# Decoder self-attention of a transformer block: another order of VectorE's row maxima and subtractions within a batch

## What is computed

```python
def _L1_attn_ref(x, w_qkv, w_proj, b_proj):      # 16 heads of 8 features
    Q, K, V = split(x @ w_qkv)
    Q, K = apply_rope(Q), apply_rope(K)
    attn = einsum('bqhd,bkhd->bhqk', Q, K) * scale
    attn = where(causal, attn, -1e9)
    attn = softmax(attn, axis=-1)
    return einsum('bhqk,bkhd->bqhd', attn, V) @ w_proj + b_proj
x = _layernorm(x + _L1_attn_ref(...))
```

## Time and profile before

| | us |
|---|---|
| runs (3) | 1361.73, 1365.23, 1362.21 |
| median | 1362.21 |
| span of the profiled execution | 1363.6 |
| PE busy / share of the span | 1199.7 / 88% |
| DVE busy / share | 1041.1 / 76% |
| ACT busy / share | 863.3 / 63% |
| POOL busy / share | 553.3 / 41% |

### The profile page before, as it was taken

How to read it: one execution, slowest core, us unless ns; L and a number is a source line. 1 busy time by engine, 2 the same in 40 slices (tenths; PEclk the granted TensorE clock), 3 DMA queues, 4 the chain that set the end, 5 groups by cost and what they waited for, 6 DMA issues and landing times. The chain is left out here.

```text
span 1363.6 us, 31925 instructions
## 1 busy us (share of the span) xinstructions
PE 1199.7 (88%) x10209; PEld 819.7 (60%) x10209; DVE 1041.1 (76%) x3184; ACT 863.3 (63%) x2474; POOL 553.3 (41%) x831
## 2 busy tenths in 40 slices
PE   3789999999999999988489988999999979999796
PEld 2456666666666666654256655555555556777796
DVE  3477888887888888885678867999999975666365
ACT  2677887878887878864246643666666654543464
POOL 1233334425353434432400017556655311556377
PEclk9999999999999999987589988999999999999899
DMA  6100000000000000000122222013100000000673
GB/s 267 52 17 9 17 15 21 29 17 29 15 31 17 26 19 17 13 15 13 53 67 81 82 71 98 24 39 79 43 24 18 5 1 3 17 17 25 178 209 92
DMA packets 71490, 63.54 MB, mean 47 GB/s; under 512 B 10510, under 2 KB 61586, under 8 KB 70688
## 3 DMA queue, kind: packets, MB, share of 16 engines
q1 hardware_dynamic: 62768, 45.27, 11.5%
q0 software_dynamic: 6400, 12.63, 3.0%
q10 hardware_dynamic: 2160, 3.60, 0.8%
HBM read 43.00 MB, written 18.98 MB: 45 GB/s over the span
## 5 line engine op out<-in xcount | busy, mean ns | idle before, releaser
L777 PE MATMUL e_bank_turned<-c_matrices,e_probs 128*128 128x128 f32 x1024 | 166.0, 286 | 16.2 <-ACT e_probs_t L1009 9.0
L703 POOL TENSOR_TENSOR e_rstd<-e_var_eps,c_minus_half 128x1 f32<-128x1 f32 x128 | 71.0, 570 | 253.6 <-DVE e_var_eps L1050 253.3
L1009 ACT ACTIVATE e_probs_t<-e_bank_turned 128x512 f32<-128x512 f32 x256 | 154.9, 605 | 16.0 <-PE e_bank_turned L777 14.5
L1137 DVE TENSOR_REDUCE e_neg_max<-e_bank_scores 128x4 f32<-128x512 f32 x160 | 109.5, 684 | 50.6 <-PE e_bank_scores L820 50.2
L777 PEld LDWEIGHTS e_bank_turned<-c_matrices,e_probs 128*128 128x128 f32 x1024 | 116.7, 145 | 39.9 <-issue 16.1
L787 PE MATMUL e_bank_mix<-e_probs_t,e_values 128*32 128x128 f32 x2048 | 113.2, 294 | 15.5 <-ACT e_probs_t L1009 15.1
L968 ACT ACTIVATE e_probs<-e_scores,e_neg_max 128x128 f32<-128x128 f32 x384 | 123.2, 410 | 1.1 <-DVE e_neg_max L1173 1.1
L1784 ACT ACTIVATE d_probs_t<-d_bank_turned 128x512 f32<-128x512 f32 x128 | 77.4, 605 | 65.9 <-PE d_bank_turned L1661 65.9
L963 ACT ACTIVATE e_probs<-e_scores 128x512 f32<-128x512 f32 x128 | 82.1, 642 | 42.0 <-DVE e_scores L1170 41.4
L706 POOL TENSOR_TENSOR e_k_by_place<-e_q_k_k,c_matrices 128x512 f32<-128x512 f32 x64 | 66.6, 1040 | 102.6 <-DVE e_q_k_k L1181 102.6
L1766 ACT ACTIVATE d_probs<-d_scores 128x512 f32<-128x512 f32 x128 | 80.8, 631 | 38.9 <-DVE d_scores L1807 38.5
(11 more groups left out here) (328 smaller groups left out, 3267.4 us busy)
## 6 DMA issues: line engine op xcount, KB each, us to landing
streamed<-in_s_up SPq DMA_DIRECT2D x36, 258.0 KB, 3.4
sorted_rows<-scratch_sorted SPq DMA_DIRECT2D x72, 64.0 KB, 1.8
scratch_expert_out<-m_y SPq DMA_DIRECT2D x72, 64.0 KB, 1.5
sorted_rows<-scratch_sorted SPq DMA_DIRECT2D x40, 65.0 KB, 3.0
e_x_in<-in_x SPq DMA_DIRECT2D x32, 64.0 KB, 1.9
e_ctx_in<-in_ctx SPq DMA_DIRECT2D x32, 64.0 KB, 2.1
up<-in_m_wgv SPq DMA_DIRECT2D x1, 2048.0 KB, 7.5
up_b<-in_m_bgv SPq DMA_DIRECT2D x1, 2048.0 KB, 14.1
```

Source lines behind the costliest of these rows:

```text
L777: last = nc.tensor.transpose(turned_bank[:, j * P:(j + 1) * P], pr[k % 3][:, j, :], c["ident"][:])
L1009: nc.scalar.activation(pt[k % 2][:], turned_bank[:], ACT.Copy).then_inc(probs_t_ready, 1)
L1137: nc.vector.tensor_reduce(nmax[k % 4][:], bank, AX.X, ALU.max, negate=True).then_inc(max_ready, 1)
```

## The change

Only DVE's queue in `phase_decode` is written in another order. The instructions are the same, and so are the semaphores that they wait for and signal; the four pairs of a batch are laid out anew over its ticks.

```diff
             for tick in TICKS:
-                if 0 <= tick < UNITS_ALL:
-                    b, g = divmod(tick, G)
-                    dve.wait_ge(scores_done, b + 1)
-                    bank = quad[:, g, :].rearrange("p (j u) -> p j u", j=G)
-                    nc.vector.tensor_reduce(nmax[tick % 4][:], bank, AX.X, ALU.max, negate=True).then_inc(max_ready, 1)
-                    dve.wait_ge(max_ready, tick + 1)
-                    if tick >= 4:
-                        dve.wait_ge(probs_ready, tick - 3)
-                    nc.vector.tensor_tensor(sc[tick % 4][:], bank, bcast(nmax[tick % 4][:], P), ALU.add).then_inc(shifted, 1)
+                inside, g = 0 <= tick < UNITS_ALL, tick % G
+                if inside and g == 0:
+                    largest(tick)
+                    largest(tick + 1)
+                    shift(tick)
+                if inside and g == 1:
+                    shift(tick)
+                    largest(tick + 1)
+                if inside and g == 2:
+                    largest(tick + 1)
+                    shift(tick)
+                if inside and g == 3:
+                    shift(tick)
                 if (b := due(tick, 8)) is not None:
                     dve.wait_ge(mix_back, b + 1)
```

More of the change, by code:

```diff
@@ L1796, in _, with bank_of, largest, shift @@
             chain = Chain(dve, links, 0, 0)
-            for tick in TICKS:
-                if 0 <= tick < UNITS_ALL:
-                    b, g = divmod(tick, G)
-                    dve.wait_ge(scores_done, b + 1)
-                    bank = quad[:, g, :].rearrange("p (j u) -> p j u", j=G)
-                    nc.vector.tensor_reduce(nmax[tick % 4][:], bank, AX.X, ALU.max, negate=True).then_inc(max_ready, 1)
-                    dve.wait_ge(max_ready, tick + 1)
-                    if tick >= 4:
-                        dve.wait_ge(probs_ready, tick - 3)
-                    nc.vector.tensor_tensor(sc[tick % 4][:], bank, bcast(nmax[tick % 4][:], P), ALU.add).then_inc(shifted, 1)
+            def bank_of(u):
+                return quad[:, u % G, :].rearrange("p (j u) -> p j u", j=G)
+            def largest(u):
+                dve.wait_ge(scores_done, u // G + 1)
+                nc.vector.tensor_reduce(nmax[u % 4][:], bank_of(u), AX.X, ALU.max, negate=True).then_inc(max_ready, 1)
+            def shift(u):
+                dve.wait_ge(max_ready, u + 1)
+                if u >= 4:
+                    dve.wait_ge(probs_ready, u - 3)
+                nc.vector.tensor_tensor(sc[u % 4][:], bank_of(u), bcast(nmax[u % 4][:], P), ALU.add).then_inc(shifted, 1)
+            for tick in TICKS:
+                inside, g = 0 <= tick < UNITS_ALL, tick % G
[11 more added lines that the diff above has]
+                    shift(tick)
                 if (b := due(tick, 8)) is not None:
```

## The result

| | kernel before | change |
|---|---|---|
| median of runs, us | 1363.61 (1361.73 to 1365.23, 4 runs) | 1380.07 (1376.17 to 1381.05, 4 runs) |
| ratio, 95% interval | | 1.0099 [1.0071, 1.0127] |
| span of the profiled execution, us | 1363.6 | 1374.3 |
| its mean granted clock | 0.964 | 0.962 |

The change is slower, by more than I forecast: 1380.07 us against 1369.5, and above my range. The other three runs of the change had a mean clock of 0.956 or 0.957. In a later comparison (experiment e5) the same kernel came out at a ratio of 1.0061 [1.0034, 1.0088]; my forecast was 1369.5 / 1362.21 = 1.0054. So the direction and the mechanism stand, and two things are missing from the sum.

The account below looks back on a forecast made before the run. PE's chain with its detour over DVE was taken as the bound. Losses of 5.3 us (batches 5 to 29), 1.0 (batches 2 to 4) and 1.0 (last two) added 7.3 to 1362.2: 1369.5 us, range 1364.0 to 1373.0.

Parts of the forecast that it names:

- What bounds the kernel: Steady batches: PE's chain with its detour over DVE's reciprocal and `d_mix` sets the 8.83 us period; faster DVE buys nothing.
- The stalls between a maximum and its subtraction: DVE's queue: four stalls of 0.11 us removed, 0.43 us of DVE time per batch, priced at nothing.
- The second maximum ahead of the reciprocal: Batches 5 to 29: reciprocal starts at 1.82 instead of 1.61 us, losing 0.21 us per batch, 5.3 us in all.
- Batches 2 to 4: Early batches: reciprocal moves from 1.50 to 1.82 us behind the first maximum, costing 3 × 0.32 = 1.0 us.
- The first subtraction: Subtraction and ACT's first exp 0.49 us later; covered in steady batches, costing 2 × 0.49 = 1.0 us in batches 30 and 31.
- What arrives earlier: Subtractions 1 to 3 and the norms' block come about 0.5 us earlier; nobody waits for them, so nothing gained.
- Rival A: DVE's queue is the bound, so the removed stalls save 12.9 us: 1349.3 us, chance 0.04.
- rival B: PE's chain absorbs the later `d_mix`; only the last batches' 1.0 us remains: 1363.2 us, chance 0.09.
- rival C: ACT's late exp costs 0.49 us in each of 30 batches, 14.7 us: 1376.9 us, chance 0.04.

Follow-up runs that it names:

- e5: The changed kernel itself, with no edit, run again in a second group beside the kernel before: 1373.08 us, ratio 1.0061.
- e9: Kernel before with only DVE reordered: reciprocal still third, rotation behind maximum 2, two of four stalls gone; PE's queue unchanged: 1363.39 us, ratio 0.9998.
- e6: Kernel before with PE's masks of banks 0 and 1 moved ahead of turn 1, bank 2's ahead of L1725: 1358.5 us, ratio 0.9949.
- e1: The change cut to one part: only the second maximum ahead of first subtraction and reciprocal, units 2 and 3 as before: 1371.25 us, ratio 1.0037.
- e7: Changed kernel with PE's masks of banks 0 and 1 moved ahead of turn 1, bank 2's ahead of L1725: 1358.69 us, ratio 0.9948.
- e10: Changed kernel with subtraction 1 moved up too, so two maxima and two subtractions precede the reciprocal: 1386.83 us, ratio 1.0171.
- e2: Changed kernel with one dummy addition on GpSimd ahead of each pair of gathers, to start them later: 1370.53 us, ratio 1.0032.
- e4: Kernel before with one dummy addition on GpSimd ahead of each pair of gathers: 1368.03 us, ratio 1.0020.
- e11: Changed kernel with a dummy GpSimd addition ahead of the gathers and five dummy PE matmuls in each of the last two batches: 1367.76 us, ratio 1.005.
- e3: Changed kernel with five dummy matmuls where PE idles in each of the last two batches: 1371.7 us, ratio 1.0038.
- e12: Kernel before with PE's masks early, DVE reordered with the reciprocal third, and a dummy GpSimd addition ahead of the gathers: 1351.92 us, ratio 0.9926.

## Why the prediction was right and wrong

**What bounds the kernel: right.** PE's chain with its detour over the reciprocal set the period, DVE did not. The Trainium skill ("Perfetto Trace Analysis", "Identifying the Most-Contended Engine") would have named DVE by its occupancy; the runs speak against it: e9 and the change relieve DVE and gain nothing, e6 moves masks on PE and gains 0.31 us per batch.

**"The stalls between a maximum and its subtraction": right**, at nothing (e9). The durations were right too: three instructions ahead put the reciprocal at 1.80, four at 2.40, so 0.60 us each, against 0.73 in a dependent pair. The Trainium skill ("VectorE: DVE Perf Modes", "The DRAIN you can't avoid") found with eight copies in a row that a semaphore after each costs nothing extra; for the pairs here the trace disagrees.

**"The second maximum ahead of the reciprocal": right.** 0.19 us per batch against 0.21 forecast, in the change, in e1 and in e7; a second dose of 0.60 came through in full (e10).

**"Batches 2 to 4": right**, 0.9 against 1.0.

**"The first subtraction": place right, size too large.** At full clock batch 30 grew by 0.29 us (e5, 8.41 against 8.12), not 0.49. The weigh did start 0.46 later, and with it turn 0; 0.2 us of it came back at ACT's copy of turn 0. In the kernel before ACT was still busy there with exp 1 (1100.79 to 1101.42), so that the copy started 0.24 us behind the end of turn 0; in e5 exp 1 was done early and the copy started 0.03 behind it. That is the earlier subtraction 1 at work, which I had priced at nothing in the next paragraph.

**"What arrives earlier" was the step that failed.** I wrote "Nothing". I had looked at who waits for the earlier results and found nobody, which holds for the masks; exp 1 came earlier to some use in batch 30 (above). GpSimd waits for the norms, though, and its gathers moved forward by 0.5 us. The change touches no instruction of GpSimd, but it shifts when they run. The second gather's end then fell 0.07 us ahead of the end of PE's queries and keys, and PE's signal for these was late by 0.45 us, 0.14 us of which reached the period: 21 × 0.14 = 3 us (2.7 against the kernel before, which has three early batches of 8.9 us itself). e2, e4, e10 and e11 show it from four sides.

**A term for the clock was missing.** The sum took the clock to be the same before and after, and by size this is the larger miss. In the profiled execution 1.6 us of batch 30 (9.98 against 8.41) and probably most of the 2.7 us from batch 31 to the end are stretches at half clock (e5 has 18 us of them there instead of 27 and takes 257.5 us instead of 261.0, the kernel before 258.2). The runs of the kernel before in the third group tell what the clock is worth: 1359.12 to 1359.29 us at a mean of 0.970, 1367.38 and 1367.45 at 0.961, some 0.9 us per thousandth. The change's other three runs in the result, at 0.956 and 0.957 against 0.962 in the profiled one, fit this with their 3.4 to 4.9 us more. An estimate from these rows: of the 16.5 us between the medians of the result, 6 are the forecast's terms as measured (25 × 0.19 + 0.9 + 2 × 0.29), 3 the held signal, and 0.0075 less clock (0.9565 against the 0.964 of the profile before) is worth some 7. For e5, whose early period is 9.12, the first two give 8 us, and 7.7 us lie between its medians. Whether the change lowers the clock is **open**. For it: low clock in batch 30 in the change, e2 and e10, which idle there, and not in the fed e3 and e11. Against it: e1 and e5 idle just as much and have none in batch 30 (8.41), e5's seven runs range over 0.958 to 0.970, and the kernel before ranges over 0.959 to 0.971 beside it. The larger ratio of the result may be no more than this spread over four runs.

Rival A fell with e9, rival B with the flat 9.02 of e11, rival C with e1 (late exp in every batch, period no longer than the reciprocal explains).

## What to carry to other kernels

When an edit makes an engine run ahead, list not only who waits for its results but whose *issue times* move, DMA queues on GpSimd included, and what these will then stand beside. Price a reordering by what it puts ahead of the one instruction through which the critical chain passes; here 0.6 us of independent DVE work cost 0.6 us per batch where the chain had no slack, and removing stalls elsewhere on DVE paid nothing. Before calling a loss of less than 1% understood, compare at equal granted clock, and more than once.

## What was unexpected of the hardware

A completion signal of PE that falls due near the end of an indirect DMA instruction on GpSimd can be held until about half a microsecond behind that end. PE itself goes on. In the change the signal of queries and keys was due 0.07 us behind the second gather's end (3.59) and came 0.49 to 0.57 behind it, in all 21 batches; the signal of the values (L1710), due 0.3 behind the end, came with it. In e4 turn 0's was due up to 0.43 us behind the end and came 0.51 to 0.60 behind. A signal that falls due while the gather still runs can be held as well: in e4 weigh 3's was due at 4.05, the gather ended at 4.20 to 4.30 in batches 5 to 14, and the signal came at 4.71 to 4.83. On time were, in all 21 batches, signals due 0.56 us behind the end or later (turn 0 before, 4.63; e10, 0.66 behind).

Nearness to the end is not enough, though. In the kernel before weigh 3's signal was due within 0.04 us of the gather's end, in e9 0.2 behind it, in e12 turn 0's 0.1 behind it, and none of them was held. Batches 3 and 4 of the change had the same gathers as the later ones and an on-time rotation (3.69), but late values (ACT's copy of them at 4.14 and 4.16, against 3.91 in batches 26 to 28). And in e2 weigh 3's signal, due 0.29 behind the end, was held in all 21 early batches (it came 0.51 to 0.63 behind), and the period stayed 9.02, since nobody stood waiting for it. What decides is open; whether the instruction, its descriptors or the transfer holds the signal was not separated.

The granted clock of one kernel differed between runs by over a hundredth, 0.957 to 0.970 for e1, and its times with it from 1365.05 to 1376.92 us. In the profile of the change three drops to 1.2 GHz, of 3.4 us each, lie between 1108 and 1147 us; in e3 one lies there, in e5 and before none up to 1150 us.
